# A decoder layer on one core: the first half of the first projection and norm moved into the last attention group

## The reference: what is computed

```
x = layernorm(x + attn(x))            # 16 heads of 16, causal, no scaling of x, output matrix WO
x = layernorm(x + xattn(x, ctx))      # 16 heads, 64 context rows per batch, biases, key mask
x = layernorm(x + moe(x))             # 16 experts, top 4, plus one shared expert
```

## Time and profile before

| | |
|---|---|
| median of 3 runs | 642.4 us (641.43 to 643.92) |
| profiled execution, its own time | 642.46 us |
| profiled execution, span from first to last instruction | 640.7 us |
| mean granted TensorE clock | 0.977 |
| busy: PE / DVE / ACT / POOL | 583.5 / 475.0 / 364.1 / 310.2 us |
| last attention group, first exp of it to the end | 269.1 to 291.9 us |
| projection and first norm | 291.9 to 340.9 us |

### The profile page before, as it was taken

The page is one execution under the profiler, slowest core; times in us unless marked ns, Lnnn a source line. Parts: engine busy times, 40 slices in busy tenths (PEclk is TensorE's granted clock), DMA queues, the critical chain, the costliest instruction groups (busy, mean ns, idle before and its releaser), DMA issues.

```text
span 640.7 us, 12791 instructions
## 1 busy us (share of the span) xinstructions
PE 583.5 (91%) x3766; PEld 356.6 (56%) x3766; DVE 475.0 (74%) x1306; ACT 364.1 (57%) x742; POOL 310.2 (48%) x395
## 2 busy tenths in 40 slices
PE   6978899999999999898879999999877999998994
PEld 2634434433343443225444777778546899998861
DVE  2388788887888889305965787776555987998896
ACT  2335366766666676782464644535315677776645
POOL 5414314142533433255587550647564777775650
PEclk9999899999999999999999998979987999999999
DMA  5967797172543710002930000212234896669957
GB/s 183 204 179 160 137 276 104 26 104 56 71 86 53 109 25 3 20 20 71 381 127 0 1 2 1 79 64 85 86 107 135 247 293 224 213 190 305 318 181 249
DMA packets 47773, 82.92 MB, mean 129 GB/s; under 512 B 12023, under 2 KB 28919, under 8 KB 45815
## 3 DMA queue, kind: packets, MB, share of 16 engines
q1 hardware_dynamic: 40844, 62.68, 39.0%
q0 software_dynamic: 6864, 19.44, 8.2%
HBM read 53.81 MB, written 32.48 MB: 135 GB/s over the span
## 4 chain that ended last, share of the span: by engine, by line
PE 53%; DVE 23%; DMA 8%; issue 5%; SPq 4%; ACT 4%; POOL 3%; POOLq 0%; DVEq 0%; ACTq 0%
DVE neg_max L986 9%; PE ps L1540 8%; PE ps L1564 8%; PE ps L1831 6%; PE ps L1521 4%; PE ps L1729 3%; PE ps L1854 3%; PE ps L1748 3%; DMA v_group<-expert_slots 3%; DMA stacks<-m_rows 2%; PE ps L1810 2%; POOL expert_slots L788 2%; PE ps L1765 2%; PE ps L1578 2%; ACT temps L831 2%
## 5 line engine op out<-in xcount | busy, mean ns | idle before, releaser
L986 DVE TENSOR_REDUCE neg_max<-ps 128x1 f32<-128x512 f32 (+3 forms) x304 | 181.5, 654 | 29.9 <-PE ps L1526 15.9
L831 ACT ACTIVATE temps<-ps 128x1024 f32<-128x1024 f32 (+1 forms) x192 | 146.4, 812 | 72.3 <-PE ps L1540 72.0
L724 POOL TENSOR_SCALAR_AFFINE_SELECT temps<-temps 128x256 f32<-128x256 f32 x128 | 52.3, 412 | 141.7 <-ACT temps L831 140.3
L1540 PE MATMUL ps<-stacks 99*128 99x512 bf16 (+3 forms) x384 | 94.3, 331 | 4.5 <-DMA stacks<-m_rows 2.9
L795 POOL DMA_INDIRECT expert_outputs<-x_T,w_o_xqkv x79 | 78.1, 988 | 32.8 <-issue 16.8
L1521 PE MATMUL ps<-stacks 96*128 96x512 bf16 (+3 forms) x320 | 86.9, 320 | 7.1 <-DVE neg_max L986 6.8
L1564 PE MATMUL ps<-temps,v_group 128*32 128x512 f32 (+3 forms) x768 | 81.8, 498 | 1.7 <-POOL temps L724 0.6
L788 POOL DMA_INDIRECT expert_slots<-x_tok,w_o_xqkv x64 | 62.5, 976 | 26.5 <-issue 17.2
L1831 PE MATMUL ps<-w_split,block_x 128*128 x474 | 71.9, 289 | 0.7 <-DVE block_x L1398 0.7
L1540 PEld LDWEIGHTS ps<-stacks 99*128 99x128 bf16 x384 | 27.2, 98 | 75.2 <-ACT temps L831 55.5
L1831 PEld LDWEIGHTS ps<-w_split,block_x 128*128 128x128 f32 x474 | 63.8, 195 | 1.1 <-issue 1.1
(11 more groups left out here) (221 smaller groups left out, 1085.2 us busy)
## 6 DMA issues: line engine op xcount, KB each, us to landing
stacks<-qk_parts SPq DMA_DIRECT2D x96, 128.0 KB
v_group<-expert_slots SPq DMA_DIRECT2D x79, 138.5 KB
qk_parts<-temps SPq DMA_DIRECT2D x6, 768.0 KB, 4.6
w_raw<-in_w SPq DMA_DIRECT2D x4, 1024.0 KB, 10.1
early_parts<-expert_outputs SPq DMA_DIRECT2D x4, 1024.0 KB, 8.1
expert_slots<-in_pad SPq DMA_DIRECT2D x16, 138.5 KB
expert_slots<-in_pad SPq DMA_DIRECT2D x1, 2077.5 KB
x_T<-in_xT SPq DMA_DIRECT2D x4, 512.0 KB, 6.3
```

The costliest lines, as they stand in the source:

```text
L724: nc.gpsimd.affine_select(diag, diag, [[0, 2], [1, P]], ALU.is_ge, zero, base=0, channel_multiplier=-1).then_inc(b_cut, 1)
L831: nc.scalar.activation(pt[:, n % 4, :, 0:w], ps[:, 2 + 2 * (n % 2):4 + 2 * (n % 2), 0:w], ACT.Exp, scale=SCALE).then_inc(b_exp, 1)
L986: nc.vector.tensor_reduce(nmx[:, c, h0:h0 + nh, i], ps[:, A_BANKS[n % 3], 0:w * nh].rearrange("p (h k) -> p h k", h=nh), axis=AX.X, op=ALU ...
L1540: last = nc.tensor.matmul(ps[:, bank, 0:w], ks[0:KM, u, 2 * pr + s, P * j:P * j + P], qs[0:KM, u, 2 * pr + s, q0:q0 + w], start=True, stop ...
```

## The change

In the last group TensorE's order gets eight "Y" steps: the output projections of tiles 0 to 7. Y 0 stands ahead of the group's first B step, Y 1 to Y 7 behind V 0 to V 6. VectorE does the whole first norm of these tiles (`first_norm((0, TB))`) in the place where it was idle, with the reciprocal of group 6's sums at t = 4; it also scales and adds group 5 before and scales group 6 behind them, which GpSimd did. GpSimd takes the eight powers between its cuts (`ROOT_BEHIND`: behind the cuts of B steps 3, 5, 7, 17, 19 and 21). Behind attention, VectorE unpacks all 20 pieces in a row, with the reciprocal of group 7's sums after 8 of them, then scales and adds group 7, then does tiles 8 to 15. TensorE transposes tiles 0 to 7 in a row with the first two query projections, then loops over tiles 8 to 15. ScalarE makes the high parts of two experts per tile at t = 10 to 15 (`W_TILE`, `W_ACT`: 12 experts as before), GpSimd the low parts from t = 11 (`W_LAG`): five experts, so eleven are left for the cross attention (steps 1 to 21).

```diff
@@ step_order
+    if g == NG - 1:
+        out.append(("Y", 0))
...
             out.append(("V", (n - 3) // 2))
+            if g == NG - 1 and (n - 3) // 2 < TB - 1:
+                out.append(("Y", (n - 3) // 2 + 1))
@@ build
-        W_TILE, W_LAG = 4, 4
-        W_ACT, W_POOL = NT - W_TILE, NT - W_TILE - W_LAG
+        W_TILE, W_LAG = 10, 1
+        W_ACT, W_POOL = 2 * (NT - W_TILE), NT - W_TILE - W_LAG
+        ROOT_BEHIND = {3: (0,), 5: (1,), 7: (2, 3, 4), 17: (5,), 19: (6,), 21: (7,)}
@@ gpsimd
+            def roots_behind(g, n):
+                if g == NG - 1:
+                    for t in ROOT_BEHIND.get(n, ()):
+                        power(t)
...
-                if g >= 2:
+                if 2 <= g < NG - 1:
                     normalise(g - 2)
                 for n in DIAG[2 * C0:]:
                     cut(g, n)
-            normalise(NG - 2)
+                    roots_behind(g, n)
...
-            for t in range(NT):
+            for t in range(TB, NT):
                 power(t)
                 if t >= W_TILE + W_LAG:
                     w_low(t - W_TILE - W_LAG)
@@ scalar
                 if W_TILE <= t < NT:
-                    w_high(t - W_TILE)
+                    w_high(2 * (t - W_TILE))
+                    w_high(2 * (t - W_TILE) + 1)
@@ vector
-            for g in range(NG):
+            for g in range(NG - 1):
                 group(g, vector_order(g))
...
+            def first_norm(tiles):
+                for t in range(tiles[0], tiles[1] + 1):
+                    if t == TB // 2:
+                        recip(NG - 2, (NG - 2) % 3)
+                    if t < tiles[1]:
+                        dve.wait_ge(y_ready, t + 1)
+                        norm_stats(t, ps[:, t % 2, 0:D], t, t % 4)
+                    if t > tiles[0]:
+                        norm_apply(t - 1, t - 1, (t - 1) % 4)
+            scale_o(NG - 3)
+            add_o(NG - 3)
+            first_norm((0, TB))
+            scale_o(NG - 2)
+            dve.wait_ge(filled, 11)
+            dve.wait_ge(kv_ready, 1)
+            for piece in range(20):
+                if piece == 8:
+                    recip(NG - 1, (NG - 1) % 3)
+                keep_kv(piece)
+            scale_o(NG - 1)
+            add_o(NG - 1)
+            first_norm((TB, NT))
@@ tensor
+            for s in range(TB):
+                turn(s)
+                if s == 4:
+                    query_projection(0)
+            query_projection(1)
+            for t in range(TB, NT + 4):
                 if t < NT:
+                    output_projection(t)
+                if TB <= t - 3 < NT:
+                    turn(t - 3)
+                if t - 4 in (NT - 5, NT - 1):
+                    query_projection((t - 4) // 4)
```

More of the change, by code:

```diff
@@ L733, in normalise, with power @@
                     nc.gpsimd.tensor_tensor(on[:, g, :], on[:, g, :], on[:, g - 1, :], ALU.add).then_inc(o_done, 1)
+            def power(n):
+                pool.wait_ge(ln_chain, 3 * n + 3)
+                nc.gpsimd.tensor_tensor(rstd[:, n % 4:n % 4 + 1], ve[:, n % 4:n % 4 + 1], half[:],
+                                        ALU.pow).then_inc(ln_pow, 1)
+            def roots_behind(g, n):
+                if g == NG - 1:
+                    for t in ROOT_BEHIND.get(n, ()):
+                        power(t)
             for g in range(NG):
@@ L754, in _ @@
                 nc.gpsimd.memset(vbd[S2 * d:S2 * d + S2, :, :, VW * d + DH:VW * d + VW], 1.0).then_inc(filled, 1)
[L756 to L759, removed]
             def w_low(e):
@@ L1038, in _, with scale_o, add_o @@
             nc.vector.tensor_scalar(mask, mask8, MASKED, None, ALU.mult).then_inc(mask_ready, 1)
-            dve.wait_ge(filled, 11)
-            dve.wait_ge(kv_ready, 1)
+            def scale_o(g):
+                dve.wait_ge(l_spread[g % 2], 64 * (g // 2 + 1))
+                dve.wait_ge(o_scaled, g)
+                nc.vector.tensor_tensor(on[:, g, :], on[:, g, :], rl[:, g % 2, :], ALU.mult).then_inc(o_scaled, 1)
+            def add_o(g):
+                dve.wait_ge(o_scaled, g + 1)
+                dve.wait_ge(o_done, g // 2)
+                nc.vector.tensor_tensor(on[:, g, :], on[:, g, :], on[:, g - 1, :], ALU.add).then_inc(o_done, 1)
             def keep_kv(n):
@@ L1545, in group @@
                                 u if kind == "V" else (g - 1) % 3, n)
+                    if kind == "Y":
+                        if n == 0:
+                            pe.wait_ge(ld_late, 16 * 16)
+                            pe.wait_ge(a_max, NA * NG)
+                            pe.wait_ge(m_row, NG)
+                        output_projection(n)
                     if kind == "M":
@@ L1549, in group, with output_projection @@
                                             mparts[:].rearrange("p s n -> p (s n)"), identb[:]).then_inc(m_T, 1)
+            def output_projection(t):
+                if t >= 2:
+                    pe.wait_ge(ln_in, t - 1)
+                pe.wait_ge(o_done, (t // TB + 1) * GB // 2)
+                for q in range(GB // 2):
+                    pair = on[:, t // TB * GB + 2 * q + 1, P * (t % TB):P * (t % TB) + P]
+                    last = nc.tensor.matmul(ps[:, t % 2, 0:D], pair, wo1[:, q, :], start=(q == 0),
+                                            stop=(q == GB // 2 - 1))
+                last.then_inc(y_ready, 1)
             def product(base, g, u, p):
@@ L1624, in _ @@
             last.then_inc(kv_ready, 1)
-            pe.wait_ge(a_max, NA * NG)
-            pe.wait_ge(o_kept, 2 * NG)
-            pe.wait_ge(m_row, NG)
             def transpose_x(t, bank):
@@ new lines, in turn, with query_projection @@
+            def turn(s):
+                pe.wait_ge(ln_done, s + 1)
+                if s >= 2:
+                    pe.wait_ge(xT_kept, s - 1)
+                transpose_x(s, 2 + s % 2)
+            def query_projection(c):
+                pe.wait_ge(xT_kept, 4 * c + 4)
+                if c == 0:
+                    pe.wait_ge(o_kept, 2 * NG)
+                for o in range(2):
+                    if c:
+                        pe.wait_ge(xq_kept, 2 * c + o - 1)
+                    for k in range(KC):
+                        last = nc.tensor.matmul(ps[:, 6 + o, :], wxq[:, k, P * o:P * o + P],
+                                                xT[:, k, CH * c:CH * c + CH], start=(k == 0), stop=(k == KC - 1))
+                    last.then_inc(xq_ready, 1)
```

48 lines of the change are left out of this document (removed).

## The result

The changed kernel took 646.31 us (median of 19 runs, 641.9 to 649.85) against 643.5 us (19 runs, 638.33 to 652.17) for the kernel before beside it: ratio 1.0055, interval 1.0032 to 1.0079. By the ratio it is slower by some 3.5 us, where 1.4 us less were forecast.

What follows compares the result with a forecast made beforehand. It took TensorE and ScalarE to bound the last group, and VectorE's chain of waits the stage behind; +4.5 (last group) - 7.4 (that stage) + 1.5 (cross attention) = -1.4 us, from 642.4 to 641.1, range 635.5 to 646.5.

Steps and rivals of the forecast that it cites:

- Part 1, size: Last attention group: eight output projections added on TensorE make it 4.5 us longer, bounds 3.8 and 6.8.
- Part 1, the step that failed: Last attention group: VectorE's norm, scaling of group 5 and addition are covered by 19.6 us of its idle time.
- Parts 2 and 3: Behind attention's new end E': tile 8's first add +15.05, last copy +35.3 with ScalarE late last, GpSimd's chain +33.4.
- Part 4: Last query projection before cross attention: 5.4 us again, bounds 3.6 and 6.9; stage 41.7 against 49.05, -7.4.
- Part 5: Cross attention: three low parts moved there hold VectorE 2 us longer once, +1.5 us, bounds 0 and 3.
- Sum: Whole kernel: +4.5 - 7.4 + 1.5 = -1.4 us, so 641.1 from 642.4.
- A: Tiles 8 to 15: copies wait for GpSimd's powers, not ScalarE; last copy +33.4, total 635.9; chance 0.33.
- B: Last group: GpSimd's powers each hold a cut and product about 0.6 us, +3.6; total 644.7 or 647.7; chance 0.19.
- C: First batch's norm runs past E', attention's new end, about 2 us: 643.1; chance 0.48 together with the forecast.

Runs made afterwards that it cites:

- e3: Changed kernel with half of the first batch's output projection left out (two of four matmuls of each Y step); ratio 0.9963 to the kernel before, last group 25.3 us.
- e1: Changed kernel with VectorE scaling and adding group 5 at tile 6 of the first norm, where GpSimd has no cuts; ratio 1.0004 to the kernel before.
- e11: The kernel before again, nothing edited, for a second profile and a comparison with itself; ratio 1.0030.
- e5: Changed kernel with unread filler matmuls (4, 8, 10) behind the transposes of tiles 13, 14, 15; ratio 0.9999 to the kernel before, last projection 3.7 us.
- e10: The kernel before with filler matmuls alone, 8 and 3 behind the transposes of tiles 14 and 15; ratio 0.9982 to the kernel before.
- e4: Changed kernel with low parts of experts 13 to 15 set to zero instead of computed; ratio 1.0001 to the kernel before, cross attention 149.4 us.
- e8: The changed kernel again, nothing edited, for a second profile and comparison; ratio 1.0056 to the kernel before, cross attention 149.5 us.
- e9: Changed kernel with the edits of e1 and e2 and shorter fillers (3, 7, 1 behind tiles 13, 14, 15); 637.56 us, ratio 0.9917 to the kernel before.
- e12: e9 with three more low parts moved into cross attention and fillers 0, 5, 1; ratio 1.0037 to the kernel before, cross attention 158.5 us.
- e2: Changed kernel with ScalarE making one high part per tile from tile 8 instead of two from tile 10; ratio 0.9965 to the kernel before.
- e6: Changed kernel with the edits of e1 and e2 together, no fillers; ratio 0.9968 to the kernel before, last projection 3.7 us.

## Why the prediction was wrong

**Part 1, size.** The changed kernel takes 5.15 us more for the last group, against 4.5, inside the bounds of 3.8 and 6.8. The power and the cuts at its end are as forecast (the last product waits 0.65 us), and so is the bound (e3). TensorE is still idle 2.1 us of the 27.9; the prediction had its idle time nearly gone.

**Part 1, the step that failed.** "The VectorE work ... is covered by 19.6 us of idle time". VectorE's idle time covers VectorE, but the prediction didn't ask what GpSimd does in that window. The scaling and the addition of group 5 stand ahead of the last group's first Y step, beside the last four cuts of group 6, and these grow by 1.0 us and the wait behind them by 1.16. The change had swapped a scaling by GpSimd, which stood between its cuts, for one by VectorE that runs beside them. Missing: +1.3 us, of which e1 takes 1.2 back. The Trainium skill (SBUF — State Buffer, Who interferes with whom), which has a VectorE instruction with two SBUF inputs and a GpSimd one that reads SBUF shut each other out, was weighed for the routing steps alone. The trace agrees with it here, where it wasn't applied: two VectorE instructions with two SBUF inputs, of 1.23 and 1.31 us, and two cuts that end just behind them. In the late tiles the application of the norm, which has one tensor and two scalars per partition as inputs, took 1.35 us instead of 0.41 beside a low part of 2.00; ScalarE was later still in the changed kernel, so nothing hung on it there.

**Parts 2 and 3, right.** +15.16 for the first addition of tile 8 (+15.05), +35.73 for the last copy (+35.3), ScalarE late last, and GpSimd's chain at +33.67 when ScalarE is relieved (+33.4).

**Part 4, wrong in size and in reach.** The last query projection took 6.2 to 6.4 us, between the 5.4 taken and the bound of 6.9; the stage came out at 43.0 to 43.2 against 41.7, so -6 instead of -7.4. The 5.4 was one profile's value: in e11 the kernel before has 6.3. The prediction had "TensorE has nothing but three transposes" for six microseconds ahead of it and still took the old value. It also priced the clock at this one instruction. The mean granted clock of the changed kernel is lower by 0.0062. Over the 116 runs of the kernel before, 0.01 of mean clock goes with 5.1 us, which makes 3.2 us; a correlation (-0.80) by itself shows no cause, but at the same clock of 0.970 the two kernels come out alike (644.3 before, 644.4 after, by straight lines through each one's runs). The cause is shown by the fillers, which act on nothing but TensorE's idle time ahead of this projection. With them the clocks are alike: 0.9742 (e5) and 0.9747 (e10), at means of 643.0 and 642.5 us (standard errors 0.9 and 0.8), and group 6, the last group, the stage and cross attention add up to within 0.5 us of each other. So the lower clock of the changed kernel, and with it about 3 us, hang on this gap.

The profiles locate only part of that. In all five profiles with the changed kernel's order up to this projection (after, e1, e3, e4, e8) the stage has 6.8 us at half clock; the kernel before has 3.4 or 6.8. A difference of 3.4 us is 0.9 us of the projection and 0.0026 of the mean clock. The other 0.0036, and some 2 us, no profile places: one or two profiles of a file are too few.

What makes cross attention 149.3 us and more, or 147.9 and less, can be seen in the traces. All fourteen start the same TensorE instructions within 0.01 us of each other for the first 45 us behind the first score matmul. Then eight of them have a stretch at half clock, from 45.7 us on: of 3.4 us in before, e4 and e8, which puts them 1.66 us behind e9, and of 6.8 us in after, e1, e3, e11 and e12, which puts them 3.34 us behind. Here are the stretch in e8, the same in the changed kernel's first profile, and the same place in e9:

```profile
386.80:390.20 3.40, 3.40 (x14) 2.50 (x12) 2.36 (x5) 0.36 (x1) 0.00 (x0) 0.50 0.02 5
390.30:397.00 6.70, 6.70 (x22) 4.94 (x21) 4.13 (x13) 1.61 (x3) 0.06 (x1) 0.50 0.00 0
380.30:387.00 6.70, 6.70 (x42) 4.86 (x41) 6.25 (x26) 1.39 (x3) 2.33 (x3) 1.00 0.00 0
```

Seven of the eight had half clock in the stage before; e12 had none. Of the six without that stretch, e2 alone had half clock in the stage. So it goes with the gap in twelve profiles of fourteen, and how the one would bring about the other, 55 us later, is not shown. The first profile of the changed kernel had two stretches more, of 6.8 and 3.4 us, which makes its 152.6.

The Trainium skill (TensorE: Matmul & The Clock Gate, HAM oscillation — how this bites in real kernels) has it that idle gaps between bursts put TensorE back to its low clock. The five profiles with 6.8 us at half clock at this gap, and none where it was filled, agree; e6, whose clock held over an unfilled gap, shows that it does not happen each time.

**Part 5, wrong.** +1.5 forecast, nothing found (e4, e8). The low parts hold one power up by 0.6 us, and that is made up. The mechanism itself is real, and in e12, with three more, it costs about 3 us.

**Sum.** +1.3 + 5.15 - 6.0 = +0.5 for what stands in the stages, against -1.4; the other 3 us go with the clock. Two steps failed: the overlap in group 6 was put at nothing, and the clock was priced at one instruction and at its old value.

**The rivals.** A's timing for GpSimd's chain was right but not for this kernel. B did not happen: VectorE's first addition in the group follows Y 0 by 1.17 us (272.80 against 271.63), and only the power behind cut 21 holds a product up (0.65 us against 0.37 before). C did not happen: the last application of the first batch ended at 300.3, ahead of E'.

## What to carry to other kernels

An engine that is free is not a free place: before a two-input VectorE operation goes there, look at what GpSimd does in the same microseconds, and who waits for it. When the last wait in front of a large block of matmuls is long, TensorE's clock is part of its price. A few matmuls whose result nobody reads can hold it: in the changed kernel they gave back 3.6 us by the ratios (e5), while in the kernel before no gain is shown (e10). They are to be cut to the length of the gap: 1 behind the last transposes did as well for the clock as 10, which were 1.5 us too many. Where single runs scatter by 1%, compare the mean clocks before explaining a difference of stages from two profiles.

## What the runs showed of the hardware

- Four cuts of 128x256 on GpSimd: 1.77 us alone, 2.77 beside two VectorE operations of 128x1024 with two SBUF inputs; VectorE's are slowed by 0.1 us or less. Beside a low part on GpSimd the loser is VectorE: 1.35 us instead of 0.41, and GpSimd's 2.00 instead of 1.95.
- The same file, in two profiles, had 15.0 and 22.4 us at half clock in cross attention (before) and 21.3 and 18.5 (after), at durations of 149.4, 150.1, 152.6 and 149.5. What half clock costs depends on where it falls: 3.4 and 6.8 us at 45.7 us behind the first score matmul cost 1.66 and 3.34 us; of 10.2 us at half clock at 102 to 104 us (e5, e6, e8, e9) about 1.3 us were left soon after, by how far the others caught up on e9.
